# One layer of attention and routed experts on one core: four gather buffers, first pieces of x by contraction chunk, another order of the shared down products, one chain of roots at the end

## The chip, the cores and the metric

One core of a Trainium2 chip runs the whole kernel in one launch. The metric is the device time of that launch in microseconds (us), median of three runs.

## The reference

Input x is 4 x 1024 rows of 512 numbers. First comes attention with 16 heads of 128, its output added to x and normalised:

```
qkv = x @ w_qkv;  scores = q @ k.T / sqrt(128);  probs = softmax(scores)
x = layernorm(x + (probs @ v) @ w_o)
```

Then a mixture of 32 experts (four chosen for a row by a router, 160 slots per expert) and a shared network of width 512, added and normalised again:

```
Y = (silu(Xp @ W_gate) * (Xp @ W_up)) @ W_down      # Xp: the 160 gathered rows of one expert
out = zeros.at[slots_token].add(Y * slots_w)
shared = (silu(x @ shared_gate.T) * (x @ shared_up.T)) @ shared_down.T
x = layernorm(x + out + shared)
```

The einsum over values is `bhqk,bhkd->bhkd`: only the column sums of probs are needed.

## The kernel before, in words

Most products are made of three passes: each operand is split into a rounded high part (written by ScalarE, `hi_...`) and the remainder (`lo_...`, VectorE or GpSimd), and high x high, high x low, low x high are added (`PASSES`). Each engine's program is written out by hand, and semaphores join them. SyncE issues the direct transfers, GpSimd the indirect ones.

**Start.** x comes transposed, in eight pieces of 128 tokens with all four contraction chunks (L523 to L526); w_q, w_k and w_v of head 0 stand behind pieces 0, 3 and 5 (`W_AFTER`). ScalarE copies each piece (L925), VectorE subtracts (L1327). `project` (L1677) makes six groups of twelve products per head, (Q, K, V) x two halves of 512 tokens; of head 0, groups 0 and 1 wait for four and for eight pieces (L1757).

**Heads.** 64 heads, by pairs: per tile t of eight, `scores` (L1692), one group of the next head's projection, VectorE's maximum (L1234), ScalarE's exponential (L887), VectorE's column sum (L1249). `out_tile` (L1715) multiplies with w_o. The very last head has no projection behind it; tiles 4 and 5 carry six products each of `gate_up(0, 0)` (L1753), the first 24 of the shared network; the other twelve come behind the pair (L1766).

**Shared network and routing.** For each of eight blocks of 512 rows, `gate_up(n, f)` (L1594) for f = 0 to 3, then `times`, `hi_hidden`, `lo_hidden` (L1195 to L1201) make the hidden values `hb`, and `down(n)` (L1626) multiplies them: tiles 0 to 3 over chunks 0 to 2 (nine products each), then the last chunk of all four tiles (three each), once lo_hidden(n, 3) is there. `add_shared` (L1203) adds each tile. Blocks 0, 2, 4, 6, 7 come before the experts, among the router's small steps, 1, 3 and 5 behind them.

**Experts.** For expert e, GpSimd gathers its rows in two halves of 80 (`gather`, L657) into one of two buffers `xg`; TensorE transposes them (L1638), then `expert_gate_up` and `expert_down`; ScalarE weighs the result (`weigh_e`, L823) into one of two buffers; GpSimd adds it to DRAM (`add`, L665), in two halves, each after all adds of the expert before have landed:

```
for e in range(E):
    if e + 4 < E:
        gather(e + 4)
    add(e)
```

TensorE runs transposes(e+2), expert_gate_up(e+1), expert_down(e). Weights come through a ring of four.

**End.** load_o(c) reads a block of the summed rows, the first of them once every add has landed (L580 to L586); load_late(c) reads the rows for blocks 1, 3 and 5, the last of them behind load_o(0) (L587). VectorE takes statistics (`stats_o`), a Newton chain for the inverse root (`scale_o`, twelve small operations, L60 to L87), ScalarE writes (`write_o`, L834), SyncE stores. Block 5 is the last, in two halves of two tiles, each with its own chain (L1500 to L1507).

Of the kernel before, what the change touches and what calls it, by code (L numbers as in the profile page):

```python
# [13 lines left out]
P = 128  # L14
NB = 512
# [87 lines left out]
def layer(nc, ctx, calls, acc, out):  # L103
# [105 lines left out]
    first_x = [x_raw]  # L209
    for buf in (ex, val):  # L210
        first_x += [buf[:, a, b * NB:b * NB + NB].rearrange("p (c t) -> p c t", c=C)
                    for a in range(2) for b in range(HALVES)]
    W_AFTER = (0, T // 2 - 1, T - 3)
# [38 lines left out]
    xg = rows_a_own[0:HALF].rearrange("p (q h d) -> p q h d", q=2, h=2)  # L252
# [72 lines left out]
    in_ex = [[sem(f"in_ex{q}{h}") for h in range(2)] for q in range(2)]  # L325
# [9 lines left out]
    dve_o, act_o = sem("dve_o"), sem("act_o")  # L335
# [7 lines left out]
    xT_dram = xT.rearrange("(c p) (n t) -> p n c t", p=P, t=P)  # L343
    gu_dram = [shared_w[r].rearrange("(c p) (n t) -> p n c t", p=P, t=P) for r in range(2)]
# [68 lines left out]
    def written(i, s):  # L413

        return finished(i, 0) if s == 1 else finished(i - 1, 1) if isinstance(i, int) else None

# [6 lines left out]
    def _(sp):  # L423
# [92 lines left out]
        def store_o(c, tiles=range(TT)):  # L516
            q = OUT_BUF[c]
            i = OUT_ORDER.index(c)
            on_sp.wait_ge(act_o, TT * i + tiles[-1] + 1)
# [59 lines left out]
        load_late(3)  # L579
        for h in range(2):  # L580
            sp.wait_ge(out_ey[h], 16 * E)
# [5 lines left out]
        load_late(5)  # L587
# [14 lines left out]
    def _(pool):  # L602
# [54 lines left out]
        def gather(e):  # L657
            on_pool.wait_ge(pe_et, 2 * (e - 1))
            on_pool.wait_ge(act_wt, e - 1)
            for h in range(2):  # L660
                pool.indirect_dma_start(xg[:, e % 2, h], None, x2_wide,
                                        bass.IndirectOffsetOnAxis(who[:, h, e:e + 1], 0),
                                        bounds_check=N - 1, oob_is_err=False).then_inc(in_ex[e % 2][h], 16)
# [53 lines left out]
        for e in range(4):  # L717
            gather(e)
        for q, times in ((1, 1), (2, 2), (6, 1), (7, 1)):
            pool.wait_ge(out_a[q], 16 * times)  # L720
        for e in range(E):
            if e + 4 < E:
                gather(e + 4)
            add(e)

    @block.scalar
    def _(act):
# [75 lines left out]
        def copy_x(e):  # L803
# [5 lines left out]
            for h in range(2):  # L809
                on_act.wait_ge(in_ex[e % 2][h], 16 * (e // 2 + 1))  # L810
            act.copy(slot_w[:, e], xg[:, e % 2, :, D + e]).then_inc(act_wt, 1)
# [17 lines left out]
        def write_o(c, tiles=range(TT)):  # L829
            q = OUT_BUF[c]  # L830
            i = OUT_ORDER.index(c)
            on_act.wait_ge(dve_o, i + 1 + (c == 5 and tiles[0] == 2))
# [4 lines left out]
        def hi_w(m, r):  # L837

            on_act.wait_ge(in_w[r], 16 * (m + 1))
            on_act.wait_ge(pe_g, G * (m - 1) + 2 * r + 2)  # L840
# [17 lines left out]
        def hi_g(m, par, g):  # L858

            r, half = divmod(g, 2)  # L860
# [1072 lines left out]
```

## Time and profile before

| | |
|---|---|
| median of three runs | 2819.82 us (2819.93, 2819.82, 2814.19) |
| the profiled execution | 2812.99 us |
| its span | 2811.3 us |
| TensorE busy | 2752.7 us (98%) |
| VectorE, ScalarE, GpSimd busy | 2186.4, 1407.5, 637.5 us |
| granted TensorE clock, mean | 0.989 |

Times in the views below count from the span's start; the profiled execution's own time is 1.7 us longer than its span. PE is TensorE, PEld its weight loads, DVE VectorE, ACT ScalarE, POOL GpSimd, SPq the queue of SyncE. A busy TensorE share of 98% leaves 58.6 us in which it idles. An L with a number is a line of the kernel before.

### The profile page before, as it was taken

What the parts mean: (1) busy time and instruction counts of PE and PEld (TensorE: products, weight loads), DVE (VectorE), ACT (ScalarE), POOL (GpSimd) and SP (SyncE); (2) the same over time, 40 slices, a digit from 0 to 9 for tenths busy, and PEclk for the clock granted to TensorE, in tenths of its full rate; (3) what the DMA queues carried; (4) which work ended last, traced back from release to release, by engine and by line L of the source; (5) the groups of instructions that cost most, each with busy time, mean ns of one, the idle gap of its engine ahead of it and who ended that gap; (6) DMA issues with size and microseconds to landing.
All of it is one profiled execution on the core that took longest, in us unless ns stands there. A gap on an engine that the chain in (4) does not pass through costs nothing.

```text
span 2811.3 us, 41829 instructions
## 1 busy us (share of the span) xinstructions
PE 2752.7 (98%) x13088; PEld 2284.4 (81%) x13088; DVE 2186.4 (78%) x3204; ACT 1407.5 (50%) x2497; POOL 637.5 (23%) x627
## 2 busy tenths in 40 slices
PE   8999999999999999999999999999999999999987
PEld 6888888888888888888888888888887788888876
DVE  5888888888888888888888888888888777433346
ACT  4555555566555555755555556555555331344424
POOL 2212121122122222221111213212111100366510
PEclk9999999999999999999999999999999989999999
DMA  3111111113111111221111113111110411478843
GB/s 117 38 35 35 36 34 37 34 34 113 37 34 37 34 34 38 64 85 35 34 34 34 35 36 108 34 37 34 37 38 27 138 49 40 159 225 233 247 134 135
DMA packets 212712, 193.53 MB, mean 69 GB/s; under 512 B 14620, under 2 KB 166172, under 8 KB 212624
## 3 DMA queue, kind: packets, MB, share of 16 engines
q1 hardware_dynamic: 202128, 180.47, 20.4%
q0 software_dynamic: 10496, 12.02, 2.1%
q8 instruction: 39, 0.64, 0.1%
q14 instruction: 49, 0.40, 0.0%
HBM read 166.41 MB, written 36.18 MB: 72 GB/s over the span
## 4 chain that ended last, share of the span: by engine, by line
PE 91%; DVE 4%; issue 2%; DMA 1%; ACT 1%; SPq 0%; POOL 0%; ACTq 0%; DVEq 0%; POOLq 0%
PE banks L1686 36%; PE banks L1701 24%; PE banks L1724 12%; PE banks L1659 5%; PE banks L1611 4%; PE banks L1672 3%; PE banks L1620 3%; PE banks L1711 2%; PE banks L1646 1%; PE banks L1542 1%; DVE colsum L1249 1%; DVE neg_max L1234 0%; PE banks L1567 0%; DMA rows_a<-x_wide 0%; DVE xt L1094 0%
## 5 line engine op out<-in xcount | busy, mean ns | idle before, releaser
L1686 PE MATMUL banks<-xt,w_sb 128*128 (+1 forms) x4608 | 1108.0, 389 | 10.4 <-DVE xt L1327 10.4
L1686 PEld LDWEIGHTS banks<-xt,w_sb 128*128 128x128 f32 x4608 | 866.1, 188 | 190.6 <-DVE xt L1327 10.9
L887 ACT ACTIVATE rows_a<-banks,neg_max 128x1024 f32<-128x1024 f32 x512 | 572.0, 1117 | 892.8 <-DVE neg_max L1234 892.4
L1234 DVE TENSOR_REDUCE neg_max<-banks 128x1 f32<-128x1024 f32 x512 | 625.8, 1222 | 285.5 <-PE banks L1701 282.5
L1701 PE MATMUL banks<-qk 128*128 128x512 f32 x3072 | 779.8, 389 | 4.6 <-ACT rows_a L887 4.6
L1701 PEld LDWEIGHTS banks<-qk 128*128 128x128 f32 x3072 | 576.1, 188 | 126.0 <-issue 3.4
L1249 DVE SCALAR_TENSOR_TENSOR colsum<-rows_a,inv,colsum 128x1024 f32<-128x1024 f32 x448 | 586.3, 1309 | 18.8 <-DVE inv L1241 1.5
L609 POOL TENSOR_TENSOR w_sb<-raws,w_sb 128x512 fp32r<-128x512 f32 x192 | 257.9, 1343 | 1205.0 <-ACT w_sb L841 1205.0
L1724 PE MATMUL banks<-wo_sb,val 128*128 128x512 f32 x1536 | 372.3, 391 | 1.4 <-DVE y_sb L1284 1.2
L1724 PEld LDWEIGHTS banks<-wo_sb,val 128*128 128x128 f32 x1536 | 285.9, 188 | 68.4 <-DVE y_sb L1284 7.9
L1611 PE MATMUL banks<-xt 128*128 128x512 f32 x768 | 194.2, 413 | 1.2 <-DVE xt L1094 1.2
L614 POOL TENSOR_TENSOR wo_sb<-wo_raw,wo_sb 128x512 fp32r<-128x512 f32 x64 | 95.7, 1497 | 414.3 <-ACT wo_sb L847 414.3
L870 ACT ACTIVATE qk<-banks 128x512 fp32r<-128x512 f32 x256 | 152.7, 596 | 60.8 <-PE banks L1686 60.8
L1611 PEld LDWEIGHTS banks<-xt 128*128 128x128 f32 x768 | 152.6, 201 | 34.6 <-DVE xt L1094 2.1
L1256 DVE SCALAR_TENSOR_TENSOR qk<-banks,qk 128x512 fp32r<-128x512 f32 x256 | 174.2, 681 | 7.1 <-ACT qk L870 7.0
L1284 DVE TENSOR_TENSOR y_sb<-y_sb,banks 128x512 f32<-128x512 f32 x256 | 163.7, 679 | 4.9 <-PE banks L1724 4.9
L841 ACT CAST w_sb<-raws 128x512 fp32r<-128x512 f32 x192 | 117.9, 614 | 0.8 <-DMA raws<-in_w_qkv 0.8
L670 POOL DMA_INDIRECT acc_rows<-rows_b,who x64 | 94.5, 1477 | 87.4 <-DMA acc_rows<-rows_b,who 60.1
L826 ACT ACTIVATE rows_b<-banks,slot_w 80x512 f32<-80x512 f32 x64 | 43.7, 683 | 117.8 <-PE banks L1672 110.2
L1277 DVE TENSOR_TENSOR val<-rows_b,val 128x1024 fp32r<-128x1024 f32 x64 | 100.9, 1577 | 0.9 <-ACT val L881 0.9
L621 POOL TENSOR_TENSOR xt<-raws,xt 128x128 f32 (+1 forms) x128 | 79.8, 654 | 84.2 <-ACT xt L855 84.2
L1672 PE MATMUL banks<-xt,ehb 128*80 128x512 f32 x384 | 97.6, 403 | 0.8 <-issue 0.8
(179 smaller groups left out, 2259.5 us busy)
## 6 DMA issues: line engine op xcount, KB each, us to landing
raws<-in_w_qkv SPq DMA_DIRECT2D x192, 256.0 KB, 2.9
wo_raw<-in_w_o SPq DMA_DIRECT2D x64, 256.0 KB, 2.8
y_sb<-in_x SPq DMA_DIRECT2D x32, 256.0 KB, 4.0
raw_own<-in_w_gate SPq DMA_DIRECT2D x16, 512.0 KB
raw_own<-in_w_up SPq DMA_DIRECT2D x16, 512.0 KB
raw_own<-in_w_down SPq DMA_DIRECT2D x16, 512.0 KB
raws<-in_xT SPq DMA_DIRECT2D x25, 256.0 KB, 2.9
x_wide<-y_sb SPq DMA_DIRECT2D x24, 256.0 KB, 3.5
```

The costliest lines, as they stand in the source:

```text
L609: pool.tensor_tensor(w_sb[:, LO, r], w_raw[:, r], rounded(w_sb[:, HI, r]), ALU.subtract)\
L870: act.activation(qk[:, par, r, HI, at], p_g[:, g % 2], ACT.Copy, scale=SCALE if r == Q else 1.0).then_inc(act_g, 1)
L887: act.activation(ex[:, t % 2], p_s[:, t % 2], ACT.Exp, bias=neg_max[:, t % 2], accum_out=rowsum[:, t % 2]).then_inc(act_e, 1)
L1234: dve.tensor_reduce(neg_max[:, t % 2], p_s[:, t % 2], AX_X, ALU.max, negate=True)\
L1249: dve.scalar_tensor_tensor(out=colsum[:], in0=ex[:, t % 2], scalar=inv[:, t % 2], in1=colsum[:], op0=ALU.mult, op1=ALU.add).then_inc(dve_p, 1)
L1256: dve.scalar_tensor_tensor(out=qk[:, par, r, LO, at], in0=p_g[:, g % 2], scalar=SCALE if r == Q else 1.0, in1=rounded(qk[:, par, r, HI, at ...
L1284: dve.tensor_tensor(y_sb[:, j], y_sb[:, j], p_o[:, j % 2], ALU.add).then_inc(dve_y, 1)
L1611: ins = pe.matmul(p_f(f % 2, r), s_gu[:, a, k, at], parts[:, PARTS_OF[u], b, k], start=(k == 0 and (a, b) == PASSES[0]), stop=(k == KC - 1 ...
L1672: ins = pe.matmul(psum[0:HALF, 6 + h], ehb[:, e % 2, a, at:at + HALF], wd_sb[:, e % 2, b, ic], start=(ic == 0 and (a, b) == PASSES[0]), st ...
L1686: ins = pe.matmul(p_g[:, g % 2], w_sb[:, a, r, c], xt_part(batch_par, b, c, half * NB, NB), start=(c == 0 and (a, b) == PASSES[0]), stop=( ...
L1701: ins = pe.matmul(p_s[:, t % 2, keys], qk[:, par, Q, a, at], qk[:, par, K, b, keys], start=((a, b) == PASSES[0]), stop=((a, b) == PASSES[-1]))
L1724: ins = pe.matmul(p_o[:, j % 2], val2[:, r, a, at], wo_sb[:, r, b], start=(r == 0 and (a, b) == PASSES[0]), stop=(r == 1 and (a, b) == PAS ...
```

## The change

1. x comes in eight pieces of one contraction chunk and 512 tokens, w_q ahead of them, w_k behind the fourth, w_v behind the last. The groups of head 0 run in the order Q and K of the first half, Q and K of the second, V of both, and each chunk's products wait for their own piece.
2. `down` runs tiles 0 to 2 as before and tile 3 whole, behind the wait for the last chunk.
3. Four gather buffers: two more lie in `qk`, over the hidden values; gathers 2 to 5 are issued before the loop, the first of these behind all early down products, and gather(e+6) stands before add(e).
4. In the last head the shared products are 8, 8, 4 and 4 in tiles 4 to 7 (behind the out_tile products in 6 and 7).
5. load_late(5) is issued before the waits for the adds.
6. At the end one chain of roots for block 5; statistics of three tiles, then of the fourth; VectorE writes tiles 0 and 1 (`write_last`), ScalarE tiles 2 and 3.

```diff
+    FIRST_ORDER = ((0, 0), (1, 0), (0, 1), (1, 1), (2, 0), (2, 1))
+    first_place = [(k % C, slice(k // C * NB, k // C * NB + NB)) for k in range(T)]
...
-    xg = rows_a_own[0:HALF].rearrange("p (q h d) -> p q h d", q=2, h=2)
+    xg_two = rows_a_own[0:HALF].rearrange("p (q h d) -> p q h d", q=2, h=2)
+    xg_more = rounded(qk[0:HALF, 0].rearrange("p r a s -> p (r a s)"))[:, 0:4 * (D + E)]\
+        .rearrange("p (q h d) -> p q h d", q=2, h=2)
+    xg = [xg_two[:, 0], xg_two[:, 1], xg_more[:, 0], xg_more[:, 1]]
+    AHEAD = len(xg)
...
+    SHARED_IN_HEAD = (range(0, 8), range(8, 16), range(16, 20), range(20, 24))
...
-        for k in range(T):
-            sp.dma_start(first_x[k], xT_dram[:, k]).then_inc(in_first[k], 16)
-            if k in W_AFTER:
-                load_w(0, 0, [W_AFTER.index(k)])
+        load_w(0, 0, [Q])
+        for k, (c, at) in enumerate(first_place):
+            sp.dma_start(first_x[k], xT_first[:, c, at]).then_inc(in_first[k], 16)
+            if k == C - 1:
+                load_w(0, 0, [K])
+        load_w(0, 0, [V])
...
         load_late(3)
+        load_late(5)
         for h in range(2):
             sp.wait_ge(out_ey[h], 16 * E)
...
         load_o(0)
-        load_late(5)
...
         def gather(e):
-            on_pool.wait_ge(pe_et, 2 * (e - 1))
-            on_pool.wait_ge(act_wt, e - 1)
+            on_pool.wait_ge(pe_et, 2 * (e - AHEAD + 1))
+            on_pool.wait_ge(act_wt, e - AHEAD + 1)
...
-        for e in range(4):
+        gather(0)
+        gather(1)
+        pool.wait_ge(pe_d, TT * len(EARLY))
+        for e in range(2, 6):
             gather(e)
...
-            if e + 4 < E:
-                gather(e + 4)
+            if e + 6 < E:
+                gather(e + 6)
             add(e)
...
+        hi_w(0, Q)
+        for k, (c, at) in enumerate(first_place):
+            if k == C:
+                hi_w(0, K)
+            if k == C + 2:
+                hi_g(0, 0, 0)
             on_act.wait_ge(in_first[k], 16)
...
+        def write_last(c, tiles):
+            q, i = OUT_BUF[c], OUT_ORDER.index(c)
+            on_dve.wait_ge(dve_o, i + 1)
+            for j in tiles:
+                ts(out_rows[q][:, j], out_rows[q][:, j], o_scale[:, i, j:j + 1], o_shift[:, i, j:j + 1],
+                   ALU.mult, ALU.add).then_inc(dve_z, 1)
...
-        stats_o(5, range(0, 2))
-        scale_o(5, 1, range(0, 2))
         add_shared(5, 2)
+        stats_o(5, range(0, 3))
         add_shared(5, 3)
-        stats_o(5, range(2, 4))
-        scale_o(5, 1, range(2, 4))
+        stats_o(5, range(3, 4))
+        scale_o(5)
+        write_last(5, range(0, 2))
...
-            for j in range(TT):
+            for j in range(TT - 1):
                 if j == 2:
                     on_pe.wait_ge(dve_f, IC * (n + 1))
                 down_part(j, range(IC - 1))
             on_pe.wait_ge(dve_h, IC * (n + 1))
-            for j in range(TT):
+            for j in range(TT - 1):
                 down_part(j, [IC - 1])
+            down_part(TT - 1, range(IC))
...
             for c in range(C):
+                if isinstance(m, int) and m == 0:
+                    on_pe.wait_ge(pool_x, C * half + c + 1)
```

TensorE, one `down`, before and in the change (`banks` is PSUM, `dve_f` and `dve_h` are what `times` and `lo_hidden` signal):

```order
L1620 MATMUL banks<-qk 128x512 [waits dve_h]
L1620 MATMUL banks<-qk 128x512 x17
L1620 MATMUL banks<-qk 128x512 [waits dve_f]
L1620 MATMUL banks<-qk 128x512 x17
L1620 MATMUL banks<-qk 128x512 [waits dve_h]
L1620 MATMUL banks<-qk 128x512 x11
```

```order
L1649 MATMUL banks<-qk 128x512 [waits dve_h]
L1649 MATMUL banks<-qk 128x512 x17
L1649 MATMUL banks<-qk 128x512 [waits dve_f]
L1649 MATMUL banks<-qk 128x512 x8
L1649 MATMUL banks<-qk 128x512 [waits dve_h]
L1649 MATMUL banks<-qk 128x512 x20
```

The second wait on `dve_h` stands behind 27 products instead of 36.

GpSimd's queue at the start of the expert stage, before and in the change (L661 and L677 are gathers, two rows of the queue per expert, L670 and L686 the adds; `act_wt` and `pe_et` say that a buffer is free):

```order
L661 DMA rows_a<-x_wide,who 80x544 [waits out_w0,out_w1,out_x1,dve_who,out_x0,pe_t]
L661 DMA rows_a<-x_wide,who 80x544 x3
L661 DMA rows_a<-x_wide,who 80x544 [waits act_wt,pe_et]
L661 DMA rows_a<-x_wide,who 80x544
L661 DMA rows_a<-x_wide,who 80x544 [waits act_wt,pe_et]
L661 DMA rows_a<-x_wide,who 80x544
L661 DMA rows_a<-x_wide,who 80x544 [waits out_a7,pe_et,out_a6,act_wt,out_a2,out_a1]
L661 DMA rows_a<-x_wide,who 80x544
L670 DMA acc_rows<-rows_b,who 4096x512 [waits act_ey] x2
```

```order
L677 DMA rows_a<-x_wide,who 80x544 [waits out_w0,out_w1,out_x1,dve_who,out_x0,pe_t]
L677 DMA rows_a<-x_wide,who 80x544 x3
L677 DMA qk<-x_wide,who 80x544 [waits pe_d]
L677 DMA qk<-x_wide,who 80x544 x3
L677 DMA rows_a<-x_wide,who 80x544 [waits act_wt,pe_et]
L677 DMA rows_a<-x_wide,who 80x544
L677 DMA rows_a<-x_wide,who 80x544 [waits act_wt,pe_et]
L677 DMA rows_a<-x_wide,who 80x544
L677 DMA qk<-x_wide,who 80x544 [waits out_a7,pe_et,out_a6,act_wt,out_a2,out_a1]
L677 DMA qk<-x_wide,who 80x544
L686 DMA acc_rows<-rows_b,who 4096x512 [waits act_ey] x2
```

Seven experts are gathered ahead of the first add instead of five, and gathers 2 and 3 wait for down products instead of transposes.

## Rows read from the trace of the kernel before

**Rows 1.** The page, part 4: the chain that ended last, by engine.
```profile
PE 91%; DVE 4%; issue 2%; DMA 1%; ACT 1%; SPq 0%; POOL 0%; ACTq 0%; DVEq 0%; POOLq 0%
```

**Rows 2.** Timeline from 0 (start us, us, engine, line, what).
```profile
4.70 0.62 ACT L841 CAST w_sb<-raws 128x512 fp32r<-128x512 f32 x1 [0.33 <-DMA raws<-in_w_qkv]
...
9.03 0.69 DVE L1327 TENSOR_TENSOR xt<-rows_a,xt 128x512 fp32r<-128x512 f32 x1 [0.20 <-ACT xt L925]
...
9.78 4.58 PE L1686 MATMUL banks<-xt,w_sb 128*128 128x512 f32 x12 [9.78 <-DVE xt L1327]
9.93 1.28 POOL L609 TENSOR_TENSOR w_sb<-raws,w_sb 128x512 fp32r<-128x512 f32 x1 [3.27 <-ACT w_sb L841]
...
15.02 13.89 PE L1686 MATMUL banks<-xt,w_sb 128*128 128x512 f32 x60 [0.66 <-DVE xt L1327]
...
28.75 1.52 PE L1701 MATMUL banks<-qk 128*128 128x512 f32 x6
```

**Rows 3.** Timeline of the last head, tiles 4 to 7 and behind.
```profile
2157.57 1.65 PE L1701 MATMUL banks<-qk 128*128 128x512 f32 x6 [0.70 <-ACT rows_a L887]
...
2175.22 1.29 DVE L1272 TENSOR_TENSOR rows_b<-v_sb,banks 128x512 f32<-128x512 f32 x2 [2.94 <-PE banks L1711]
```

**Rows 4.** Timeline of down(3).
```profile
2384.15 7.13 PE L1620 MATMUL banks<-qk 128*128 128x512 f32 x30 [0.52 <-DVE raws L1197]
2386.22 0.69 DVE L1201 TENSOR_TENSOR qk<-raws,qk 128x512 fp32r<-128x512 f32 x1
```

**Rows 5.** Waits from 2390 to 2700 us: us in total, times, longest.
```profile
POOL acc_rows L670 <- DMA acc_rows<-rows_b,who: 60.1, 22, 4.4
...
PE banks L1646 <- issue: 6.7, 4, 3.8
```

**Rows 6.** Timeline of the expert stage, and its busy time by windows (last column GB/s).
```profile
2440.93 1.51 POOL L670 DMA_INDIRECT acc_rows<-rows_b,who  x1 [2.13 <-ACT rows_b L826]
...
2500.36 1.45 POOL L670 DMA_INDIRECT acc_rows<-rows_b,who  x1 [1.68 <-DMA acc_rows<-rows_b,who]
...
2563.39 3.05 PE L1672 MATMUL banks<-xt,ehb 128*80 128x512 f32 x12
...
2571.11 3.05 PE L1672 MATMUL banks<-xt,ehb 128*80 128x512 f32 x12
...
2686.07 1.40 POOL L670 DMA_INDIRECT acc_rows<-rows_b,who  x1 [3.41 <-DMA acc_rows<-rows_b,who]
...
2692.54 1.40 POOL L670 DMA_INDIRECT acc_rows<-rows_b,who  x1 [3.35 <-DMA acc_rows<-rows_b,who]
...
2440.00:2500.00 60.00, 59.62 (x407) 52.01 (x406) 20.35 (x31) 30.07 (x64) 36.44 (x28) 1.00 0.87 263
2500.00:2560.00 60.00, 58.72 (x394) 50.34 (x393) 18.97 (x30) 28.86 (x61) 39.11 (x32) 1.00 0.81 237
```

**Rows 7.** Timeline of the join behind the experts, and one DMA issue.
```profile
2697.84 0.36 SPq L514 DMA_DIRECT2D rows_c<-acc_rows  x1
...
2703.48 2.47 DVE L1076 BATCH_NORM_STATS2 bn<-rows_c 128x6 f32<-128x512 f32 x4 [7.66 <-DMA rows_c<-acc_rows]
...
2709.93 1.94 PE L1542 MATMUL banks<-ident,raw_own 128*128 128x128 f32 x8 [5.80 <-DVE xt L1094]
...
2729.48 5.75 PE L1611 MATMUL banks<-xt 128*128 128x512 f32 x24 [0.62 <-DVE xt L1094]
...
rows_b<-x_wide SPq DMA_DIRECT2D x1, 1024.0 KB, 4.8
```

**Rows 8.** Timeline of the end, and an operation of tensor by scalars.
```profile
2786.76 11.04 PE L1620 MATMUL banks<-qk 128*128 128x512 f32 x48
...
2789.87 0.69 DVE L1201 TENSOR_TENSOR qk<-raws,qk 128x512 fp32r<-128x512 f32 x1 [0.69 <-ACT qk L792]
...
2806.48 1.52 ACT L834 ACTIVATE y_sb<-y_sb,o_shift,o_scale 128x512 f32<-128x512 f32 x2 [3.73 <-DVE o_shift L1087]
...
36.31 0.75 DVE L1246 TENSOR_SCALAR colsum<-rows_a,inv 128x1024 f32<-128x1024 f32 x1
```

More of the change, by code:

```diff
@@ L324, in layer @@
     out_ey = [sem(f"out_ey{h}") for h in range(2)]
-    in_ex = [[sem(f"in_ex{q}{h}") for h in range(2)] for q in range(2)]
+    in_ex = [[sem(f"in_ex{q}{h}") for h in range(2)] for q in range(AHEAD)]
     dve_who = sem("dve_who")
@@ L415, in written, with group @@
         return finished(i, 0) if s == 1 else finished(i - 1, 1) if isinstance(i, int) else None
+    def group(m, g):
+        return FIRST_ORDER[g] if isinstance(m, int) and m == 0 else divmod(g, 2)
+    SHARED_IN_HEAD = (range(0, 8), range(8, 16), range(16, 20), range(20, 24))
     def x_piece(k):
@@ L518, in store_o @@
             i = OUT_ORDER.index(c)
-            on_sp.wait_ge(act_o, TT * i + tiles[-1] + 1)
+            if c == 5 and tiles[0] == 0:
+                on_sp.wait_ge(dve_z, 2)
+            else:
+                on_sp.wait_ge(act_o, TT * i + tiles[-1] + 1 - (2 if c == 5 else 0))
             at = slice(tiles[0], tiles[-1] + 1)
             sp.dma_start(rows_of(out_v, c)[:, at], out_rows[q][:, at]).then_inc(out_o[q], 16)
-        for k in range(T):
-            sp.dma_start(first_x[k], xT_dram[:, k]).then_inc(in_first[k], 16)
-            if k in W_AFTER:
-                load_w(0, 0, [W_AFTER.index(k)])
+        load_w(0, 0, [Q])
[4 more added lines that the diff above has]
+        load_w(0, 0, [V])
         load_w(1, 1)
@@ L831, in write_o @@
             i = OUT_ORDER.index(c)
-            on_act.wait_ge(dve_o, i + 1 + (c == 5 and tiles[0] == 2))
+            on_act.wait_ge(dve_o, i + 1)
             for j in tiles:
@@ L839, in hi_w @@
             on_act.wait_ge(in_w[r], 16 * (m + 1))
-            on_act.wait_ge(pe_g, G * (m - 1) + 2 * r + 2)
+            on_act.wait_ge(pe_g, G * (m - 1) + (3 if isinstance(m, int) and (m, r) == (1, Q) else 2 * r + 2))
             act.copy(w_sb[:, HI, r], w_raw[:, r]).then_inc(act_w, 1)
@@ L858, in hi_g @@
         def hi_g(m, par, g):
-            r, half = divmod(g, 2)
+            r, half = group(m, g)
             at = slice(half * NB, half * NB + NB)
@@ L1053, in _ @@
         write_o(3)
-        write_o(5, range(0, 2))
         write_o(5, range(2, 4))
@@ L1252, in lo_g @@
         def lo_g(m, par, g):
-            r, half = divmod(g, 2)
+            r, half = group(m, g)
             at = slice(half * NB, half * NB + NB)
@@ L1323, in _ @@
         dve.tensor_copy(ones[:], ones_f).then_inc(dve_1, 1)
-        for k in range(T):
-            at = slice(k * P, k * P + P)
+        for k, (c, at) in enumerate(first_place):
+            if k == C + 2:
+                lo_g(0, 0, 0)
             on_dve.wait_ge(act_x, k + 1)
-            dve.tensor_tensor(xt[:, 0, LO, :, at], first_x[k], rounded(xt[:, 0, HI, :, at]),
+            dve.tensor_tensor(xt[:, 0, LO, c, at], first_x[k], rounded(xt[:, 0, HI, c, at]),
                               ALU.subtract).then_inc(pool_x, 1)
-        for g in range(4):
+        for g in range(1, 4):
             lo_g(0, 0, g)
@@ L1677, in project @@
         def project(m, par, g, batch_par):
-            r, half = divmod(g, 2)
+            r, half = group(m, g)
             on_pe.wait_ge(pool_w, 3 * m + r + 1)
@@ L1751, in pair @@
                         turn(0, 2 * s + 1)
-                    if is_last(i) and s == 1 and t in (4, 5):
-                        gate_up(0, 0, range(6 * (t - 4), 6 * (t - 3)))
+                    if is_last(i) and s == 1 and t >= 4:
+                        gate_up(0, 0, SHARED_IN_HEAD[t - 4])
         for g in range(G):
-            if g < 2:
-                on_pe.wait_ge(pool_x, T // 2 * (g + 1))
             project(0, 0, g, 0)
@@ L1764, in _ @@
         pair(PAIRS - 1)
-        gate_up(0, 0, range(12, 24))
         gate_up(0, 1)
```

38 lines of the change are left out of this document (17 added, 21 removed).

## The prediction, made before the changed kernel was run

> **What bounds the kernel now.** I read the chain of work that ended last first [rows 1]: 91% of it is TensorE, so time is won only where TensorE idles, or at the ends of the program, where something else ends last. The change leaves the loop over the heads as it is. So I went through the timeline at the places that it touches. At the start TensorE waits until 9.78 us for the fourth piece of x and again 0.66 us for the eighth; the first group takes 4.58 us, each of the other five 2.75 (a fifth of 15.02 to 28.75), and the first scores begin at 28.75 [rows 2]. In the last head VectorE holds TensorE back by 0.70 us before a tile of scores [rows 3]. In the expert stage the list of waits has two things to see: TensorE stood 6.7 us in four gaps before the transposes of gathered rows, but GpSimd waited 60.1 us for scatter-adds to land [rows 5]. At the join, load_o(0) is issued at 2697.84, when the last scatter-add has landed; VectorE stood 7.66 us for its rows; TensorE stood 5.80 us behind that [rows 7]. At the end, VectorE and ScalarE work 10.2 us (2797.8 to 2808.0) after the last product [rows 8].
>
> **The start.** The same bytes arrive in the same order but for three swaps: w_q goes first, x comes in contraction chunks instead of token blocks, and w_v goes behind the last x. Chunk 0 is now cast where w_q was, at 4.70, and with 0.62 and 0.69 for the two operations subtracted by 6.1 [rows 2], where TensorE can begin instead of at 9.78; w_q is ready before it. The fourth piece still ends its subtraction at 9.72 [rows 2], and three products follow it: the first group ends at about 10.6. The second needs w_k, whose low part is ready at 11.21 (9.93 + 1.28) as before. Its twelve products take 2.75 us at full rate or, if the clock is still low, 4.58, what the first group took before. TensorE will have run in pieces for 5 us by then, so I take 3.1: 14.3. Four groups of 2.75 follow without a wait, since the eighth piece, ready at about 15.0 before, comes earlier with w_v behind it; first scores at 25.3. **Gain 3.5.** At the two rates the second group ends at 13.95 or 15.8: gain 3.8 or 2.0. The rows show the first twelve products 382 ns apart and later ones 229: most of the first group ran at the lower level of the clock, 1.2 GHz, after 9.8 us of idling. The Trainium skill, TensorE: Matmul & The Clock Gate, Part 1, says that the throttled clock is the default and that activity releases it. Read against this change, a first group broken by waits for chunks would not release it, and the gain would be the 2.0; if broken activity counts, 3.8.
>
> **The last head.** Twelve products of gate_up(0, 0), 2.7 us, move in from behind the pair: two more in each of tiles 4 and 5, four each in 6 and 7. Behind tiles 4 and 5 TensorE idles 0.7 us each (tile 5's gap stands in [rows 3], tile 4's is the same), so 2 x 2 x 0.23 = 0.9 us is hidden. Tiles 6 and 7 have out_tile products back to back, so these eight only move; tile 7's scores come 0.9 later and VectorE's last maximum some 0.6 later, which its 2.94 us of idling before times_v covers [rows 3]. **Gain 0.9**, between 0 (VectorE passes its delay on) and 2.0 (the gap behind tile 3 too).
>
> **The order of down.** Tile 3 now runs whole after the wait for the last chunk, so tiles 0 to 2 end after 30, 33 and 36 products instead of 39, 42 and 45, 9 x 0.23 = 2 us earlier. But the wait stands after 27 products instead of 36. In down(7) the low part is ready 3.8 us after the start (2786.76 to 2790.56 [rows 8]), before 27 products have run (6.1), and down(5) and down(6) have the same steps ahead: no cost. In down(3) the 27 end at 2384.15 + 9 x 0.23 = 2386.2, and the subtraction L1201 ends at 2386.91 [rows 4]: **a new stall, 0.75 us** (18 products ran until 2388.3 before); TensorE is not waiting anywhere between there and the experts, so it stays (0.7 to 0.9). Behind down(5), and as long behind down(6), TensorE waits 0.62 us for L1094, which stands behind the first two additions [rows 7]; these come 2 us earlier: **gain 1.25** (the two waits, no more). The other early downs have no wait behind them that an earlier addition would end: 0.
>
> **Four gather buffers.** GpSimd issues gather(e+6) before add(e) instead of gather(e+4), after the same transposes(e+2). So gathers are two experts, 15 us, ahead, and the gaps (6.7 us) and a slow stretch behind the longest (1.3) should go: 8.0. But the scatter-adds are a chain of their own: each waits for the landing of the one before. From 2440.93 to 2692.54 there are 31 periods, 8.12 us each, where TensorE's own period is 7.72 (2563.39 to 2571.11) [rows 6]. load_o(0) waits for this chain, not for TensorE [rows 7]. The buffers don't shorten an add. TensorE will run ahead until ScalarE's weigh_e(e), which needs add(e-2), holds it, and wait longer at the join: some 6 to 8 us reappear there. What is left: two more periods at the end have no gather behind their adds; the last of all, with no gather and no weights either, took 6.47 [rows 6], 1.65 less than the mean. **Gain 0.8**, a quarter of twice that, between 0 and 8.0 (as if TensorE set the end). In front, gathers 2 to 5 wait for down(4) and are issued by about 2437, gather(6) by 2440: the first add, at 2440.93, keeps 0.9 us of cover. load_late(5) leaves the place behind load_o(0) and runs among the last adds: load_o(0) took 5.6 us, the quickest load of its size 4.8 [rows 7]: **gain 0.3**, 0 to 0.8, and up to 0.8 lost if it slows the adds instead.
>
> **The end.** One chain of roots, twelve operations each 0.197 us apart, instead of two. From down(7)'s start at 2786.76 the first three tiles are ready at 2793.7, 2794.4 and 2795.1; additions until 2795.8, three statistics 1.9, aggregation 0.5: 2798.3. Tile 3 was ready at 2797.9: addition 0.7, statistics 0.7, aggregation 0.3: 2800.0; roots 2.4: 2802.4. ScalarE writes two tiles in 1.52: 2804.0, against 2808.0 [rows 8]. VectorE writes the other two in 0.75 (L1246 takes that for as many elements), so their store starts at 2803.3. The second store alone would end the program 3.3 us after its rows, as before: 2807.3, gain 4.0. If the two together take the 4.8 of a load of 1 MB [rows 7], with 0.4 behind a landing: 2808.5, gain 2.8. **Gain 3.5**.
>
> **Sum:** 3.5 + 0.9 - 0.75 + 1.25 + 0.8 + 0.3 + 3.5 = 9.5 us. The profiled execution took 2812.99 (span 2811.3): it would take 2803.5. The median of the three runs shown lies 6.8 above it, their lowest 1.2: I subtract the 9.5 from the median, **2810.3**, and keep the lower level for the range. A measurement of this kernel can tell about 0.2%, 5.6 us, from no change.
>
> **Rivals.**
> (A) TensorE sets the end of the expert stage, and the adds keep up. For it: after a gap its products run slow and everything behind shifts; all adds share one queue with the gathers, which would now be out of their way. Against: 60.1 us of GpSimd's waits name the adds' landing. It adds 8.0 - 0.8 = 7.2: 2803.1.
> (B) Denser traffic slows the adds. For it: the first seven periods, at 263 GB/s, took 8.49 us each (2440.93 to 2500.36), the other 24 took 8.01, at 237 where they begin [rows 6]. With TensorE's 8 us of 247 gone, weights are asked for 3% faster, 8 GB/s, at 0.48 / 26 us per GB/s 0.15 us per add, 4.6 us over 31. Against: TensorE can be ahead by two experts at most, so over the stage the traffic keeps the adds' pace. At 0.31 us per add the whole gain is gone; from 0.49 (15.1 / 31) the kernel is slower by over 0.2%. The 0.15 alone gives 2814.9; the whole 0.48 that the stretches differ by, 14.9 us, and the 0.8 of load_late(5) among the adds give 2826.0, slower than before. The Trainium skill (Trainium Kernel Development and Optimization, Key Constraints) says that transfers issued from SP, ACT and POOL run on the same 16 engines and interleave; by that rule buffers add no bandwidth, and the trace's 8.12 above 7.72 agrees.
> (C) Most terms come out at their low ends: the clock stays low at the start, the last head hides nothing, the adds gain nothing from fewer gathers and lose 0.8 to load_late(5). 2.0 + 0 - 0.9 + 1.25 + 0 - 0.8 + 2.8 = 4.35: 2815.5. For it: the granted clock and the landings depend on when work falls, and all of it shifts; against: the terms are separate, each with its own rows.
>
> **Chances.** The forecast 0.56; A 0.13; B 0.11, of which 0.05 beyond its second point; C 0.20, 0.07 of it with over 5.6 us left. Faster: 0.56 + 0.13 + 0.07 = 0.76; within 0.2%: 0.13 + 0.06 = 0.19; slower 0.05. The range: below, A from the lowest run shown is 2814.2 - 16.7 = 2797.5, of which I leave the last part out: 2799. Above, C's 2815.5 and the half of B in which the adds take back up to all of the gain: 2819.
>
> **What would show it.** First scores at about 25.3. A wait of 0.7 us inside down(3). No gap before transposes in the expert stage, but adds still 8.1 apart, ScalarE (L826 of before) waiting for their landing, load_o(0) issued at about 2693.4 (3.5 + 0.9 - 0.75 + 0.8 before 2697.84), and TensorE standing 10 us or more before L1542 there in place of 5.80. No 0.62 waits behind down(5) and down(6). About 6.2 us, not 10.2, from the last product to the last write, with one chain of roots. Adds 7.8 apart would make A right, 8.4 B; first scores after 26.5, C.

## The result, and the profile after

The changed kernel takes 2798.34 us (median of 11 runs, 2793.82 to 2805.41), the kernel before 2815.75 (11 runs, 2808.70 to 2819.93). The ratio is 0.9948, 95% interval 0.9936 to 0.9960: **14.6 us faster (11.3 to 18.0)**, where 9.5 were forecast. This is the ratio turned into us; the two medians themselves lie 17.4 us apart, and where the two ways of comparing differ, both numbers are given below. The forecast of 2810.3 also started from a median of three runs that lay 4.1 us above that of eleven. 2798.3 falls 0.7 us below the range.

| | before | after |
|---|---|---|
| median of 11 runs | 2815.75 us | 2798.34 us |
| the profiled execution, and its span | 2812.99, 2811.3 us | 2804.82, 2803.1 us |
| first scores | 28.75 | 25.55 |
| down(3) begins | 2379.28 | 2377.52 |
| first transposes of gathered rows | 2426.88 | 2424.78 |
| load_o(0) issued | 2697.84 | 2693.57 |
| down(5), down(7) begin | 2717.82, 2786.76 | 2714.80, 2781.90 |
| from the first product of down(7) to the end | 24.5 us | 21.2 us |

The two profiled executions lie only 8.2 us apart. That of after (2804.82) is near the top of its 11 runs, that of before (2812.99) below the median of its own, so stages are compared below over all traces that have the same stage. The chain that ended last, by engine, has less of TensorE and more of DMA than before [rows 1], since the scatter-adds are now a part of it:

```profile
PE 89%; DVE 4%; DMA 3%; issue 2%; ACT 1%; POOL 1%; SPq 0%; POOLq 0%; ACTq 0%; DVEq 0%
```

The timeline of after, from the start, the last head and down(3) (start us, us, engine, line, what):

```profile
6.54 19.18 PE L1718 MATMUL banks<-xt,w_sb 128*128 128x512 f32 x72 [6.54 <-DVE xt L1356]
...
12.15 0.60 ACT L889 ACTIVATE qk<-banks 128x512 fp32r<-128x512 f32 x1 [1.31 <-PE banks L1718]
...
14.87 0.60 ACT L889 ACTIVATE qk<-banks 128x512 fp32r<-128x512 f32 x1 [1.10 <-PE banks L1718]
...
25.55 1.52 PE L1733 MATMUL banks<-qk 128*128 128x512 f32 x6
...
2154.79 1.65 PE L1733 MATMUL banks<-qk 128*128 128x512 f32 x6 [0.26 <-ACT rows_a L906]
...
2384.08 5.10 PE L1649 MATMUL banks<-qk 128*128 128x512 f32 x21 [0.28 <-DVE qk L1229]
```

TensorE starts 3.2 us earlier, and the timeline shows no further idle time of it up to the first scores: the first group ends at about 12.1 (its result is copied at 12.15), the second 2.72 later [rows 2]. The gap behind tile 4 and that behind tile 5 shrank from 0.69 and 0.70 to 0.20 and 0.26 [rows 3]. In down(3) the new wait behind 27 products is there, 0.28 us long, and the old one of 0.52 behind 18 [rows 4] is not. The order isn't the reason that the old one went: the 24 products ahead of down(3) took 7.18 us in this execution and 5.71 in that of before, which gives VectorE more time. Where they take 5.7, as in x1, x4 and x5 below, both waits stand; in x4's list (us in total, times, longest):

```profile
PE banks L1649 <- DVE raws L1225: 0.5, 1, 0.5
PE banks L1649 <- DVE qk L1229: 0.5, 1, 0.5
```

In the expert stage (waits between 2390 and 2700: us in total, times, longest):

```profile
POOL acc_rows L686 <- ACT rows_b L845: 39.6, 11, 5.8
POOL acc_rows L686 <- DMA acc_rows<-rows_b,who: 36.8, 15, 4.1
ACT rows_b L845 <- DMA acc_rows<-rows_b,who: 32.0, 13, 4.3
...
PE banks L1702 <- issue: 2.0, 4, 0.8
...
PE banks L1676 <- issue: 1.2, 1, 1.2
```

Of the 6.7 us in four gaps before the transposes (now L1676) one of 1.2 is left. Instead ScalarE waits 32.0 us for landings before it weighs rows (3.1 before): TensorE is so far ahead that both buffers of weighed rows are in use. This differs from one four-buffer trace to the next: 11.5 us in x4, none in x2. The join, from the timeline:

```profile
2682.89 1.41 POOL L686 DMA_INDIRECT acc_rows<-rows_b,who  x1 [5.75 <-ACT rows_b L845]
...
2689.30 1.41 POOL L686 DMA_INDIRECT acc_rows<-rows_b,who  x1 [3.29 <-DMA acc_rows<-rows_b,who]
...
2693.57 0.36 SPq L525 DMA_DIRECT2D rows_c<-acc_rows  x1
...
2699.16 2.47 DVE L1097 BATCH_NORM_STATS2 bn<-rows_c 128x6 f32<-128x512 f32 x4 [11.26 <-DMA rows_c<-acc_rows]
...
2705.62 1.94 PE L1571 MATMUL banks<-ident,raw_own 128*128 128x128 f32 x8 [9.40 <-DVE xt L1122]
2707.21 7.75 PE L1640 MATMUL banks<-xt 128*128 128x512 f32 x24
```

The chain is that of [rows 7], with a longer wait: TensorE stands 9.40 us (5.80 before) for lo_t(3, 0), which stands in VectorE's queue behind the statistics of rows that the last scatter-add has to precede. The 24 products behind it take 7.75 us, at a mean granted clock of 0.72 of 2.4 GHz (2707.2 to 2715); the same 24 take 5.6 elsewhere. The 9.40 is not what four buffers usually leave: the wait is 5.78 in x2 and 5.65 in x10, and 5.68 to 5.99 in the two-buffer traces with this order. In the profiled execution of the change one of the last adds took 2.4 us longer than in most traces (see load_late(5) below).

The end:

```profile
2781.90 11.04 PE L1649 MATMUL banks<-qk 128*128 128x512 f32 x48
...
2797.43 1.52 ACT L853 ACTIVATE y_sb<-y_sb,o_shift,o_scale 128x512 f32<-128x512 f32 x2 [6.49 <-DVE o_shift L1115]
2797.43 1.00 DVE L1107 TENSOR_SCALAR y_sb<-y_sb,o_scale,o_shift 128x512 f32<-128x512 f32 x2
```

From the last product (2792.94) to the last write (2798.95) it is 6.0 us, 10.2 before [rows 8].

### The profile page after: what moved, and what is told of

Same layout as the page of the kernel before. It is cut to its first block, busy times and chain, and to the rows that moved or that the text cites. A ratio compares the mean times of both kernels' runs of the same rounds, so it can differ in the third digit from the quotient of the medians.

```text
span 2803.1 us, 41819 instructions
## 1 busy us (share of the span) xinstructions
PE 2755.0 (98%) x13088; PEld 2287.4 (82%) x13088; DVE 2185.9 (78%) x3194; ACT 1405.3 (50%) x2495; POOL 637.9 (23%) x627
## 4 chain that ended last, share of the span: by engine, by line
PE 89%; DVE 4%; DMA 3%; issue 2%; ACT 1%; POOL 1%; SPq 0%; POOLq 0%; ACTq 0%; DVEq 0%
PE banks L1718 36%; PE banks L1733 24%; PE banks L1756 12%; PE banks L1640 4%; PE banks L1689 3%; PE banks L1649 3%; DMA acc_rows<-rows_b,who 2%; PE banks L1702 2%; PE banks L1743 2%; PE banks L1571 1%; DVE colsum L1277 0%; POOL acc_rows L686 0%; PE banks L1676 0%; PE banks L1596 0%; DVE neg_max L1262 0%
## 5 line engine op out<-in xcount | busy, mean ns | idle before, releaser
L1640 PEld LDWEIGHTS banks<-xt 128*128 128x128 f32 x768 | 152.9, 201 | 32.9
L686 POOL DMA_INDIRECT acc_rows<-rows_b,who x64 | 92.6, 1446 | 89.7 <-ACT rows_b L845 39.6
```

The lines of the kernel that those rows point to most:

```text
L1640: ins = pe.matmul(p_f(f % 2, r), s_gu[:, a, k, at], parts[:, PARTS_OF[u], b, k], start=(k == 0 and (a, b) == PASSES[0]), stop=(k == KC - 1 ...
```

## The experiments

Twelve kernels ran, each timed beside the kernel before on the same chip (its medians there 2814.56 to 2815.83). Theory: the chain of scatter-adds ends the expert stage, and what TensorE wins there it loses at the join. Rival A: TensorE sets the end. The measured column is the ratio to the kernel before, turned into us at its median, with the interval. "Stage" is from the first transposes of gathered rows to the issue of load_o(0) in the one profiled execution, "adds" the mean of its 31 periods.

| | buffers | ratio to before | us | stage | adds |
|---|---|---|---|---|---|
| before | 2 | 1 | 0 | 271.0 | 8.12 |
| the change | 4 | 0.9948 | -14.6 (-18.0, -11.3) | 268.8 | 7.95 |
| x1 two buffers | 2 | 0.9961 | -11.0 (-14.6, -7.3) | 271.8 | 8.09 |
| x2 buffers only | 4 | 0.9979 | -5.9 (-9.0, -3.1) | 263.1 | 7.82 |
| x3 half the adds | 4 | 0.9919 | -22.8 (-26.5, -19.1) | 257.6 | 7.71 |
| x4 join | 4 | 0.9906 | -26.5 (-30.4, -22.2) | 263.3 | 7.83 |
| x5 join, two buffers | 2 | 0.9938 | -17.4 (-21.4, -13.2) | 267.9 | 8.02 |
| x6 join on before | 2 | 0.9982 | -5.1 (-8.2, -1.7) | 270.6 | 8.05 |
| x7 start, old waits | 2 | 1.0011 | +3.1 (+0.3, +6.2) | 271.8 | 8.10 |
| x8 end only | 2 | 0.9988 | -3.4 (-5.9, -0.6) | 270.1 | 8.05 |
| x9 start | 2 | 0.9977 | -6.5 (-9.6, -3.7) | 273.8 | 8.17 |
| x10 half the gathers | 4 | 0.9917 | -23.4 (-27.9, -18.9) | 261.6 | 7.83 |
| x11 join, old down | 4 | 0.9918 | -23.1 (-26.8, -19.1) | 263.1 | 7.82 |
| x12 join, best | 4 | 0.9883 | -32.9 (-37.2, -28.7) | 265.5 | 7.94 |

### The buffers: x1 and x2

x1 takes them away from the change, x2 adds them alone to the kernel before.

```diff
-    xg = [xg_two[:, 0], xg_two[:, 1], xg_more[:, 0], xg_more[:, 1]]
+    xg = [xg_two[:, 0], xg_two[:, 1]]
...
-        gather(0)
-        gather(1)
-        pool.wait_ge(pe_d, TT * len(EARLY))
-        for e in range(2, 6):
+        for e in range(4):
             gather(e)
...
-            if e + 6 < E:
-                gather(e + 6)
+            if e + 4 < E:
+                gather(e + 4)
```

> The changed kernel with two gather buffers again (everything else of the change kept). Theory (the chain of scatter-adds ends the expert stage, TensorE's lead is only moved to the join): the four gaps before the transposes come back (6 to 8 us of TensorE's idling), adds 8.0 to 8.1 us apart, load_o(0) issued 1 to 2 us later, and the wait at the join shrinks from 9.4 to 4 or 5 us; total 0.8 to 2.5 us above the changed kernel's 2798.3, so about 2800. Rival (TensorE sets the end of the stage): the gaps come back in full, 7 to 8 us above, about 2806.

> The kernel before with the four gather buffers alone, and the later start of gathers that comes with them. Theory: 0.8 to 2.5 us below the kernel before's 2815.8, about 2814; no gaps before transposes, the wait at the join 10 us or more in place of 5.8. Rival (TensorE sets the end): 7 to 8 us below, about 2808. If the missing 5 us of my forecast lie in this part, it takes 5 us or more off.

x2 gained 5.9 us and x1 lost 3.6 (6.6 by medians) against the change: about 5 us, more than the 0.8 of the theory and less than the 8 of the rival. The gaps behave as expected (x1 has them again: 2.7, 1.5, 0.5 and 1.2 us, beside the first of 1.2; x2 only the first, 1.2). The wait at the join does not: 5.99 in x1, where 4 or 5 were expected, and 5.78 in x2, where 10 or more were. So in x2 what TensorE wins in the gaps does not come back at the join, against the theory: the stage itself is shorter. Over all traces, two buffers give 267.9 to 273.8 us, mean 271.0 (seven); four give 263.1 to 268.8, mean 264.8 (five, without x3 and x10): **6.2 us**. Only the trace of the change itself is close to the two-buffer ones: its first add comes 17.9 us behind the first transposes (15.1 to 15.5 in the other four), and one of its last takes 2.4 us longer. What became shorter is the period of the adds, 8.08 against 7.87 us. The timeline of x2:

```profile
2444.75 1.51 POOL L674 DMA_INDIRECT acc_rows<-rows_b,who  x1 [1.16 <-ACT rows_b L833]
...
2687.04 1.41 POOL L674 DMA_INDIRECT acc_rows<-rows_b,who  x1 [3.44 <-DMA acc_rows<-rows_b,who]
...
2692.33 0.36 SPq L518 DMA_DIRECT2D rows_c<-acc_rows  x1
...
2704.39 1.94 PE L1549 MATMUL banks<-ident,raw_own 128*128 128x128 f32 x8 [5.78 <-DVE xt L1101]
```

31 periods in 242.3 us are 7.82 each, against 251.6 in the kernel before [rows 6].

### Are the adds still the bound? x3 and x10

x3 leaves out the scatter-add of the second half of each expert's rows. x10 leaves out the gather of the second half, so stale rows are computed there.

```diff
         def add(e):
             for h in range(2):
                 on_pool.wait_ge(act_ey, 2 * e + h + 1)
-                for g in range(2):
-                    on_pool.wait_ge(out_ey[g], 16 * e)
+                if h == 1:
+                    continue
+                on_pool.wait_ge(out_ey[0], 16 * e)
...
         def gather(e):
-            for h in range(2):
+            for h in range(1):
```

(The second piece is x10's alone; the waits of the left out halves are dropped in both.)

> The changed kernel with one scatter-add per expert in place of two: the adds of the second half of each expert's rows are left out, so half of the routed experts' contribution is missing from the output. Theory (the chain of adds ends the stage): the adds then follow TensorE, 7.73 us apart, load_o(0) is issued 6 us earlier relative to the last expert_down, and the wait at the join falls from 9.4 to 3 or 4 us; total 5 to 7 us below the changed kernel, about 2792. Rival (TensorE sets the end): nothing changes, 2798 within 2.

> The changed kernel with one gather per expert in place of two: the rows of the second half of each expert's slots are not gathered, so the output is computed from stale rows there. It measures what a gather costs the scatter-adds. Theory (each gather's traffic and issue lengthen the add that runs beside it; the two more gather-free adds of the change were worth 1.2 us each): the landing of an add, 7.06 us beside two gathers and 5.7 to 6.0 beside none, falls to 6.4 to 6.6, the adds keep TensorE's pace of 7.73, and the total is 4 to 7 us below the changed kernel, 2791 to 2794. Rival (the adds' time is their own and the weight loads', gathers don't matter): landings stay at 7.0 and the total within 2 us of the changed kernel.

x3 is 8.2 us below the change by ratios, 6.4 by medians, and its stage 7.2 us under the mean of the four-buffer ones. In its waits between 2390 and 2700 GpSimd hardly waits for landings any more (x10 below it, for comparison):

```profile
POOL acc_rows L687 <- ACT rows_b L847: 98.2, 28, 6.6
...
POOL acc_rows L687 <- DMA acc_rows<-rows_b,who: 9.7, 2, 6.5
```

```profile
POOL acc_rows L686 <- DMA acc_rows<-rows_b,who: 73.0, 21, 5.3
...
ACT rows_b L844 <- DMA acc_rows<-rows_b,who: 25.8, 13, 3.3
```

TensorE waits 1.6 us at the join in x3. So the adds do end the stage in the changed kernel, and with half of them 31 periods take 238.9 us, 7.71 each, at TensorE's pace (244.1 over the four-buffer traces). Of the 7.2 us 5.2 are these periods; 1.2 is that load_o(0) follows the last issue sooner (3.6 us against 4.8) and 0.8 the first add. By the stage, four buffers took 6.2 us of the 13.4 between two buffers and x3. x3 takes bytes off the DMA engines as well as steps off the chain; which of the two counts it can't say.

x10 refutes my explanation of the shorter period. I had made it: less traffic of gathers, quicker adds. With half of the gathers the adds came 7.83 apart, like the 7.82 to 7.95 with all. From issue to landing the 24 middle ones take 7.2 us, where 6.4 to 6.6 were expected and 7.0 to 7.1 stand in the four-buffer traces. The rival of that run holds for the adds. The total fell all the same, by 3.3 us by medians and 8.8 by ratios; in the stage, 3.2 us under the mean of the four-buffer ones, 1.4 is the first add, which comes 14.05 us behind the first transposes and not 15.5 as in x2. The gap of 1.2 before the third transposes is missing in x10; fewer gathers in front may be the reason, but the kernel before has the 14.05 with all of them.

### The wait at the join: x4, x6 and x5

The theory says that TensorE's lead is there, but lost in a wait for work that VectorE has behind the statistics. x4 changes VectorE's order in the changed kernel, x6 in the kernel before; x5 is x4 with two buffers.

```diff
         share_step(5, 0)
-        stats_o(0)
         share_step(5, 1)
         lo_t(3, 0, True)
         lo_t(3, 1, True)
         share_step(5, 2)
-        stats_o(2)
+        stats_o(0)
         share_step(5, 3)
+        stats_o(2)
```

> The changed kernel with VectorE's order at the join changed: the statistics of the first loaded rows (which wait for the last scatter-add and a load) stand behind share_step(5, 1), lo_t(3, 0), lo_t(3, 1) and share_step(5, 2) instead of ahead of them. Theory (TensorE's lead ends in a wait for VectorE, which waits for rows that TensorE doesn't need yet): the 9.4 us wait before the transposes goes, and the following 24 products take 5.6 us in place of 7.75 at the lower clock: 9 to 11.5 us below the changed kernel, about 2788. Rival (the loads behind the last add bound what follows anyway): TensorE waits behind down(5) for the additions to loaded rows, and less than 4 us are gained, 2795 or more.

> The kernel before with the order of VectorE at the join changed as in x4, nothing else. Theory: the wait of 5.80 us goes, and the slow products behind it (6.46 us in place of 5.6) get faster: 5.5 to 7 us below the kernel before, about 2808. Rival: VectorE's additions behind down(5) wait for loads, 2 us or less.

> The kernel of x4 (statistics behind share_step(5, 2) at the join) with two gather buffers in place of four. Theory now (two buffers cost TensorE gaps of 6 to 7 us before the transposes; the adds' chain hides part of them as long as TensorE waits for it at the join): with no wait at the join the gaps count in full, 6 to 8 us above x4's 2789.7, about 2797. Rival (the chain of adds sets the end here too, since the rows behind the join must wait for it): 2 us or less above x4.

x4 is 8.6 us below the change by medians, 11.9 by ratios. Its timeline at the join:

```profile
2681.46 11.15 PE L1640 MATMUL banks<-xt 128*128 128x512 f32 x48
...
2686.52 0.36 SPq L525 DMA_DIRECT2D rows_c<-acc_rows  x1
...
2692.45 1.04 PE L1571 MATMUL banks<-ident,raw_own 128*128 128x128 f32 x8
2693.24 5.73 PE L1640 MATMUL banks<-xt 128*128 128x512 f32 x24
2698.81 11.04 PE L1649 MATMUL banks<-qk 128*128 128x512 f32 x48
```

No wait is left, and the 24 products take 5.73 us, not 7.75. From load_o(0) to down(5) it is 12.3 us in place of 21.2. The loads held nobody. x6 gives 5.1 us on the kernel before, where the wait was 5.80. With the join no longer waiting, x5 is 9.0 us above x4 (9.3 by medians), where 6 to 8 were expected. In the traces 4.9 us of gaps stand against the one of 1.3, and from the first transposes to down(5) it is 280.5 against 275.6: 4.9 us. The rest of the 9 is not in this stage, and no trace explains it. By medians and ratios the buffers are worth 3.6 to 6.6 us with the old join (x1, x2) and 9 with the new one, and the join 5.1 us on the kernel before (x6), 6 on x1 (x5 against it) and 8.6 to 11.9 on the change. That the two edits help each other is likely from this, but the intervals of some 3.5 us on either side of each number overlap: it is not shown.

### The start, the end and the order of down: x7, x9, x8, x11

> The kernel before with the start of the change alone (first pieces of x by contraction chunks, w_q first, order of the first groups). First scores at 25.4 to 25.6 in place of 28.75, as in the changed kernel; total 3.2 below the kernel before, and the expert stage as in the kernel before: adds 8.1 apart, TensorE's gaps back, some 271 us from the first transposes to the issue of load_o(0). If that stage comes out at 265 or less here, the gain that I read for four buffers is scatter between runs.

x7 was not the edit that this text describes: it kept the two waits ahead of the first two groups, for the fourth and the eighth subtraction, which the change drops. So it shows the order of the pieces without the finer waits:

```profile
9.60 5.49 PE L1701 MATMUL banks<-xt,w_sb 128*128 128x512 f32 x12 [9.60 <-DVE xt L1340]
...
17.70 15.49 PE L1701 MATMUL banks<-xt,w_sb 128*128 128x512 f32 x60 [2.61 <-DVE xt L1340]
33.03 1.30 PE L1716 MATMUL banks<-qk 128*128 128x512 f32 x5
```

The first scores come 4.3 us later than in the kernel before: the new order with the old waits is a loss. x9 has the order and the finer waits.

> The kernel before with the whole start of the change: as x7, and without the two waits that stood in front of the first two groups (there the fourth and the eighth subtraction, here one subtraction per chunk). Theory: first product at 6.5, first scores at 25.5 (28.75 before, 33.03 in x7), total about 3 below the kernel before's 2814.6; the expert stage is the kernel before's, 268 to 272 us from the first transposes to load_o(0).

```profile
6.56 18.82 PE L1701 MATMUL banks<-xt,w_sb 128*128 128x512 f32 x72 [6.56 <-DVE xt L1340]
25.22 1.52 PE L1716 MATMUL banks<-qk 128*128 128x512 f32 x6
```

First scores at 25.2; over the nine traces with this start they come at 24.9 to 25.8, mean 25.3, over the four with the old one at 28.8 to 29.4, mean 29.0: 3.7 us. The total fell by 6.5 (3.7 to 9.6), where 3 were expected; nothing in its trace says where the rest comes from. That x9's profiled stage of 273.8 is the longest and its total is not, says how far one trace may be from the median.

> The kernel before with one chain of roots and the split last write alone, down in its old order. By the durations of the profiles the last write ends 19.0 us after the first product of down(7), against 21.2 before and 17.05 in the changed kernel: 2.2 of the 4.2 us come from the chain and the split, 2.0 from the order of down. The expert stage is the kernel before's again: 271 us from the first transposes to load_o(0).

> The kernel of x4 with the order of down of before in all eight. Theory from the durations: the two waits of 0.62 us behind down(5) and down(6) come back (1.2), the last write ends 19.0 us after the first product of down(7) in place of 17.05 (2.0), and the wait inside down(3) of 0.5 goes: 2.7 us above x4, about 2792.5. Rival: the order is worth nothing, since VectorE's statistics end last either way; 2789.7.

```diff
-            for j in range(TT - 1):
+            for j in range(TT):
                 if j == 2:
                     on_pe.wait_ge(dve_f, IC * (n + 1))
                 down_part(j, range(IC - 1))
             on_pe.wait_ge(dve_h, IC * (n + 1))
-            for j in range(TT - 1):
+            for j in range(TT):
                 down_part(j, [IC - 1])
-            down_part(TT - 1, range(IC))
```

Both by their own rows. In x8 the last write begins at 2806.32 and ends 19.1 us after the first product of down(7) (2788.75): the 19.0 expected. In x11 (x4 with this edit) the waits behind down(5) and down(6) are back and the last write ends 19.1 us after down(7) began:

```profile
2704.54 5.75 PE L1640 MATMUL banks<-xt 128*128 128x512 f32 x24 [0.62 <-DVE xt L1122]
...
2761.81 11.04 PE L1649 MATMUL banks<-qk 128*128 128x512 f32 x48
...
2779.38 1.52 ACT L853 ACTIVATE y_sb<-y_sb,o_shift,o_scale 128x512 f32<-128x512 f32 x2 [8.55 <-DVE o_shift L1115]
```

By medians x11 is 2.6 us above x4, by ratios 3.4. So one chain and the split last write are worth 2.2 us, and the order of down about 3: 2.0 of them at the end, which the forecast had put under the chain, and 1.25 for the two waits, less 0.5 in down(3).

### The best version: x12

x4, with expert_gate_up(1) ahead of transposes(2), and the old order of down in the five early ones.

```diff
         for e in range(E):
+            if e == 0:
+                expert_gate_up(1)
             if e + 2 < E:
                 transposes(e + 2)
-            if e + 1 < E:
+            if 0 < e and e + 1 < E:
                 expert_gate_up(e + 1)
```

> The kernel of x4, with expert_gate_up(1) ahead of transposes(2), which in x4 and the others wait 1.2 us for their gathers, and the old order of down in the five early ones alone, where it has no 0.5 us wait inside down(3). Theory: 1.3 + 0.5 = 1.8 us below x4, about 2788; no wait of TensorE over 0.5 us between 2380 and the end but that of 0.82 before the last products of the experts. Rival: the later transposes(2) delay gather(6) and the first adds, which then hold TensorE somewhere in the stage; 2790 or more.

2784.40 us, 32.9 below the kernel before and 7.9 below x11 in the same comparison, where 4.5 were expected (2.7 + 1.8); against x4 it is 5.3 by medians and 6.4 by ratios, where 1.8 were expected. Its trace doesn't explain the excess: its stage of 265.5 us is 2.2 longer than x4's, and its two edits were not run apart. TensorE's waits between 2390 and 2710 are down to

```profile
PE banks L1704 <- issue: 0.8, 1, 0.8
PE banks L1678 <- ACT exT L827: 0.3, 1, 0.3
```

## Why the prediction was right in direction and too small

- **Start, 3.5.** Measured 3.7 over the traces. Not by the steps given, and errors partly cancelled: the first group ended at 12.1, not 10.6, and the second took 2.72 us, not 3.1, without the wait for w_k until 11.2. The pieces of x were not late (the fourth was ready at 9.50; 9.72 were forecast). The forecast had left three products to run behind the fourth piece, but the first ten of the twelve ran 0.43 us apart, against 0.23 in the second group, so at the lower level of the clock, with a single break of some 0.25 us (11 products begin in 4.8 us from 6.5, 13 in the next 2.7); six or seven had begun when the last piece came. The rule of the Trainium skill (TensorE: Matmul & The Clock Gate, Part 1: activity releases the clock) agrees with the second group's full rate. Whether activity with longer breaks counts too, the forecast's other question, this execution doesn't show: its first group was hardly broken.
- **Last head, 0.9.** gate_up(0, 3) began 4.1 us earlier with 3.2 from the start: 0.9.
- **Order of down.** The stall in down(3) was forecast at 0.75 on top of the old 0.52. It is 0.48 on top of it in x1, x4 and x5, and 0.28 without it here, behind slower products: 0.5 lost. The waits of 0.62 went, 1.25 as forecast.
- **load_late(5), 0.3.** load_o(0) took 5.6 us as before: nothing gained. In two executions it cost something, as the forecast had allowed with up to 0.8. In the change the load is issued at 2675.17, 1.2 us behind an add (2674.00), and the next add follows 8.9 us after that one. x12 has the same:

```profile
2669.51 1.41 POOL L686 DMA_INDIRECT acc_rows<-rows_b,who  x1 [4.62 <-ACT rows_b L845]
...
2670.55 0.36 SPq L520 DMA_DIRECT2D raw_own<-x_wide  x1
...
2678.45 1.41 POOL L686 DMA_INDIRECT acc_rows<-rows_b,who  x1 [5.82 <-ACT rows_b L845]
```

In x4 the load comes 3.4 us behind an add, and the next add after 6.5:

```profile
2668.18 1.41 POOL L686 DMA_INDIRECT acc_rows<-rows_b,who  x1 [4.53 <-issue]
...
2671.57 0.36 SPq L520 DMA_DIRECT2D raw_own<-x_wide  x1
...
2674.69 1.41 POOL L686 DMA_INDIRECT acc_rows<-rows_b,who  x1 [3.39 <-ACT rows_b L845]
```

In x1, x5, x10 and x11 it comes 3.1 to 3.7 us behind one. This period is 6.3 to 6.6 us in all other traces with two adds per expert. So the load seems to cost 2.4 us when it falls right behind an add; no run moves it alone, so that is not shown.

- **End, 3.5.** 3.3 from the first product of down(7) to the end of the span; x8 and x11 split it as above.
- **Gathers, 0.8: the step that failed.** In the profiled execution all the signs were there: the gaps gone, ScalarE waiting for landings, load_o(0) at 2693.57 (2693.4 forecast), TensorE standing 9.4 us at the join (10 or more forecast). Two of them are luck. load_o(0) hit because only 2.1 us of the gain ahead of the stage were left at its start, where 3.65 were forecast, and the stage brought 2.2 and not 0.8. The 9.4 goes with the one slow add; in x2 the wait is 5.78, as without the buffers, so the 6 to 8 us that should reappear there did not. The step was "The buffers don't shorten an add", with the mean of 8.12 us taken as an add's fixed price and the two more gather-free periods discounted to a quarter. Measured: 7.87 over five traces against 8.08 over seven, 0.21 less, 6.5 us in 31. Of these 2.6 are the 26th and 27th period, in which no gather runs now (6.9 us against 8.2), the price that I had read off the last add and then quartered. The other 3.9 are 0.13 in each of the rest; as the means of single periods differ by -1.0 to +1.6 us between the two kinds, this split is a reading and not shown. The landings say more. From the issue of an add's first half to the landing of its second it is 7.10 us in the mean of the two-buffer traces and 6.92 in that of the four-buffer ones; from there to the next issue 0.99 and 0.95. So 5.5 of the 6.5 us are quicker landings, and only 1.0 is less waiting of adds for products that TensorE brought late. Why an add lands sooner I can't explain.
- **Rival A** (adds 7.8 apart, 2803.1, 16.7 us below the median) has the period nearly right and the total nearer than the forecast. It is wrong that TensorE sets the end: x3 takes another 6 to 8 us off by thinning the adds. The forecast's other half, that the lead reappears at the join, is as wrong for x2. **Rival B** is refuted: TensorE did ask for more, 254 GB/s in the changed kernel between 2442 and 2640 against 247 before (2440 to 2640), and the adds got quicker. **Rival C** fell with first scores at 25.3 and the end's 3.3.
- **The sum** by measured terms: 3.7 + 0.9 - 0.5 + 1.25 + 6.2 + 3.3 = 14.9, against 14.6 (11.3 to 18.0) measured. The 6.2 is the difference of two means of traces; x1 and x2 put the buffers at 3.6 to 6.6. A few us of scatter are left in such a sum.

What stays open: why an add beside two gathers lands 0.14 us sooner with four buffers (7.15 against 7.28 us over the first 25). x10 speaks against the gathers' bytes: with half of them the adds landed no sooner. Weights traffic was not taken away in any run.

## What to carry to other kernels

When two chains run beside each other at nearly the same pace (7.7 and 8.1 us), the mean period of the slower is not a fixed price: here it fell by 0.21 us with an edit that doesn't touch that chain, most of it in the landings. A small change of a period has to be multiplied by the number of periods, 31 here, before it is left out of a sum. Thin out the bound itself for one run (x3) to see what is left below it. And where an improvement reappears as a wait, look at what stands in the queue ahead of the awaited instruction: moving two calls of VectorE's behind work that TensorE needed took another 8.6 to 11.9 us off, beside the 14.6 of the whole change.

## What the runs showed of the hardware

The routing, from turn(1, 0) to the first transposes of gathered rows, has the same instructions in every kernel here but for down's order (new in x5, old in x11), yet took 223.9 us in x11 and 232.4 in x5 by the profile, with a mean granted clock of 0.92 and 0.89 of 2.4 GHz (windows; the column behind POOL's busy time is the clock, the last GB/s):

```profile
2193.49:2417.41 223.92, 214.80 (x1361) 183.78 (x1360) 167.46 (x542) 54.55 (x107) 16.16 (x17) 0.92 0.20 68
```

```profile
2194.26:2426.70 232.44, 220.96 (x1362) 188.62 (x1360) 168.13 (x542) 54.73 (x107) 16.18 (x17) 0.89 0.20 66
```

That is as much as most single edits bring. The start's gain had shrunk from 4.1 to 2.1 us behind this stage in the profiled pair, by the clock.

From one expert's pair of scatter-adds to the next it is 6.5 us when little else moves, and 7.9 beside the gathers and the loads of the weights. The adds of x2 show both; 24 of them fill the first of these windows:

```profile
2454.85:2645.13 190.28, 190.28 (x1278) 165.14 (x1277) 64.83 (x99) 93.34 (x195) 123.26 (x97) 1.00 0.88 252
...
2666.34:2687.04 20.70, 19.88 (x111) 15.88 (x110) 5.81 (x10) 8.38 (x15) 8.44 (x7) 1.00 0.38 49
```

At 252 GB/s a period is 7.93 us; at 49 the last two are 6.48 and 6.56 (2674.00, 2680.48, 2687.04).
